# Cross attention of a two-layer decoder, written out as one row of 32 rounds with new bank shares and a later layer norm

## The chip, the cores and the metric

The kernel runs on one core of one Trainium2 chip. The time is the device time of one execution in microseconds (us); the kernel before took 2605.74 us, the median of three runs (2604.7 to 2606.8). An engine takes its instructions strictly in the order in which they stand in its own queue and waits on semaphores for the others. TensorE (PE; PEld is its loading of weights) multiplies into eight banks of PSUM, each 128 x 512 fp32; ScalarE (ACT) and VectorE (DVE) read the banks; GpSimd (POOL) works in SBUF only; SyncE (SP) issues the DMAs.

## The reference

Four sequences of 512 tokens of width 512 pass six blocks, each `x = layernorm(x + f(x))`. The fifth is the one touched:

```
# x [4, 512, 512], ctx [4, 512, 256]; 16 heads of width 128
q = (x @ Wq).reshape(B, Sq, H, D);  k = (ctx @ Wk).reshape(...);  v = (ctx @ Wv).reshape(...)
q = rmsnorm(q, gq);  k = rmsnorm(k, gk)
attn = softmax(einsum('bqhd,bkhd->bhqk', q, k) / sqrt(D))
out = einsum('bhqk,bkhd->bqhd', attn, v).reshape(B, Sq, H * D) @ Wo
x = layernorm(x + out)
```

## The kernel before, in words

The stages run one after another, with a barrier of all engines between. `cross_attention` takes two heads at a time: 8 groups of heads for each of 4 sequences, 32 rounds. Its precision comes from splitting: each fp32 operand is a high part (fp32r, a ScalarE copy) and a low part (the difference), and `split3` (L196) makes three products hi*hi, hi*lo, lo*hi.

A round has these parts, named as the changed code names them:

- **Q**: queries of 2 x 128 columns, two banks of 2 x 256, 24 products each. ScalarE squares and copies each bank (L1833, L1836); VectorE sums the squares (L1909) and scales the result (L1912); GpSimd raises it to -1/2 (L1799, "rstd"); VectorE multiplies q by it (L1919).
- **KV**: keys and values, four tiles; ScalarE empties each in three instructions, squares, k, v (L1844, L1847, L1848). The keys' rstd enters as the scale of the exponential.
- **TQ, TK**: q and k of each head turned by TensorE (L2014, four 128 x 128 transposes to a bank), high part by ScalarE (L1853), low part by VectorE (L1939, L1942).
- **E**: scores, four tiles of 128 keys for each head; ScalarE's exponential goes to SBUF (L1862). No maximum is subtracted, a bound from the gains stands in for it.
- **U, SU**: GpSimd adds the head's four tiles (L1808, L1810), TensorE adds over partitions by a product with ones (L2038).
- **V**: the values times the probabilities (L2031). **R**: VectorE takes the reciprocal of the sum and multiplies the bank of V by it (L1925, L1928).
- **OH**: high and low part of that (L1874, L1932). **O**: four tiles of the output projection, added to x by VectorE (L1958).
- **W**: weights of the next but one round: a DMA into a raw tile, high part by ScalarE, low part by GpSimd (L1792).

The order is written by hand, as the body of a loop that works on round y and on the projections of round y+1: E of both heads, V0, Q0, SU0, V1, SU1, Q1, KV, O0, TK, TQ, O1 to O3. Hardware loops (`turns`, L1734) go over sequences and groups. Q, KV, TK, TQ and xT share banks 0 to 2 in turn, E and O banks 3 to 5, the sums use 3 and 4, V has 6 and 7. At each new sequence `start` turns x (loaded into `x_cur` by a DMA) and splits it, and splits the context; `finish` makes the layer norm on VectorE (L1978, `dve_normalize`, L334).

Of the kernel before, what the change touches and what calls it, by code (L numbers as in the profile page):

```python
# [1632 lines left out]
def cross_attention(c):  # L1633
# [8 lines left out]
    nc, d = c.nc, c.d  # L1642
    HP = 2
    G = 16 // HP
    NW = HP * DX
    with ExitStack() as ctx:
        def sb(nm, shape, dt=F32):
            return ctx.enter_context(nc.sbuf_tensor(f"s5_{nm}", shape, dt))

# [21 lines left out]
        sq = sb("squares", [P, T, NW])  # L1671
# [11 lines left out]
        consts = c.sem("s5_gains_loaded")  # L1683
        bound_ready = c.sem("s5_bound_ready")
        rawx_in = Count(c.sem("s5_w_proj_loaded"), 48)
        rawo_in = Count(c.sem("s5_w_out_loaded"), 16)
        wx_hi = Count(c.sem("s5_w_proj_hi_ready"), 1)
        wx_lo = Count(c.sem("s5_w_proj_lo_ready"), 1)
        wo_hi = Count(c.sem("s5_w_out_hi_ready"), 1)
        wo_lo = Count(c.sem("s5_w_out_lo_ready"), 1)  # L1690
        ctx_in = Count(c.sem("s5_ctx_loaded"), 16)
        ctx_hi = Count(c.sem("s5_ctx_hi_ready"), 1)
        ctx_lo = c.s5_ctx_lo
        squared = {"q": Count(c.sem("s5_q_squared"), 1), "k": Count(c.sem("s5_k_squared"), 1)}
        ms_ready = {"q": Count(c.sem("s5_q_mean_sq_ready"), 1), "k": Count(c.sem("s5_k_mean_sq_ready"), 1)}
        rs_ready = {"q": Count(c.sem("s5_q_rstd_ready"), 1), "k": Count(c.sem("s5_k_rstd_ready"), 1)}
        q_normed = Count(c.sem("s5_q_normed"), 1)
        f_hi = {"qT": Count(c.sem("s5_qT_hi_ready"), HP), "kT": Count(c.sem("s5_kT_hi_ready"), HP)}
        p_sum = Count(c.sem("s5_probs_summed"), HP)
        inv_ready = Count(c.sem("s5_inv_sums_ready"), HP)  # L1700
        o_hi = Count(c.sem("s5_out_hi_ready"), HP)


        pa, pb = c.ps.part(), c.ps.part()
        pa_keys = [("q", 0), ("q", 1)] + [("kv", t) for t in range(T)] + [("kT", 0), ("kT", 1), ("qT", 0), ("qT", 1)]
        pa.open([(k, i % 3, 1) for i, k in enumerate(pa_keys)], outer=c.x_uses([0, 1, 2]))
# [12 lines left out]
        def load_proj(sp, g):
            sp.dma_start(raw_x[:, OQ:OKV].rearrange("p (k n) -> p k n", k=KD),  # L1720
                         d["l1x_wq"].rearrange("(k p) n -> p k n", p=P)[:, :, bass.ds(g * NW, NW)]).then_inc(rawx_in.sem, 16)
            kv = raw_x[:, OKV:].rearrange("p (k a n) -> p k a n", k=KC, a=2)
            for a, nm in ((0, "l1x_wk"), (1, "l1x_wv")):
                sp.dma_start(kv[:, :, a, :],
                             d[nm].rearrange("(k p) n -> p k n", p=P)[:, :, bass.ds(g * NW, NW)]).then_inc(rawx_in.sem, 16)

        def load_out(sp, g):
            sp.dma_start(raw_o[:, :].rearrange("p (h n) -> p h n", h=HP),
                         d["l1x_wo"].rearrange("(h p) n -> p h n", p=P)[:, bass.ds(g * HP, HP), :]).then_inc(rawo_in.sem, 16)

        def turns(eng, start, body, finish):

            start(0)
            body(0, (0, 0), None)  # L1734
            with eng.Fori(0, B - 1) as b:
                with eng.Fori(0, G - 1) as g:
                    body(b, (b, b * G + (g + 1)), b * G + g)
                start(b + 1)
                body(b, (b + 1, b * G + G), b * G + (G - 1))
                finish(b)  # L1740
            b = B - 1
            with eng.Fori(0, G - 1) as g:
                body(b, (b, g + (b * G + 1)), g + b * G)
            body(b, None, b * G + (G - 1))
            finish(b)

        @block.sync
        def _(sp):
            sp.dma_start(gains[:, 0, :], d["l1x_gq"].broadcast_to([P, DX])).then_inc(consts, 16)
# [3 lines left out]
            load_proj(sp, 0)  # L1753
            load_out(sp, 0)

            def next_proj(turn, g):

                sp.wait_ge(*wx_lo.after(turn, 1))
                load_proj(sp, g)

            def next_out(turn, g):
                sp.wait_ge(*wo_lo.after(turn, 1))
                load_out(sp, g)

            def load_sequence(b):
                c.sync_load_x(sp, b)

                sp.wait_ge(*ctx_lo.after(b, 0))
                sp.dma_start(cT[:, :, :], d["ctxT"][bass.ds(b, 1)].rearrange("a (k p) s -> p (a k) s", p=P)) \
                  .then_inc(ctx_in.sem, 16)  # L1770

            load_sequence(0)
            next_proj(0, 1)
            with sp.Fori(0, B - 1) as b:
                load_sequence(b + 1)
                with sp.Fori(0, G - 1) as g:
                    next_out(b * G + g, g + 1)
                    next_proj(b * G + g + 1, (g + 2) % G)
                next_out(b * G + (G - 1), 0)
                next_proj(b * G + G, 1)  # L1780
            with sp.Fori(0, G - 1) as g:
                next_out(g + (B - 1) * G, g + 1)
                next_proj(g + ((B - 1) * G + 1), (g + 2) % G)
            next_out(B * G - 1, 0)

        @block.gpsimd
        def _(pool):
            def lo(out, raw, hi, hi_ready, done, turn, piece=None):

                pool.wait_ge(*hi_ready.after(turn, 1))  # L1790
                pool.wait_ge(c.pool_consts, 1)
                pool.tensor_tensor(out, raw, hi.bitcast(F32), ALU.subtract).then_inc(done.sem, 1)  # L1792

            lo(wx_l[:, 0, :], raw_x[:, :], wx_h[:, 0, :], wx_hi, wx_lo, 0)
            lo(wo_l[:, 0, :], raw_o[:, :], wo_h[:, 0, :], wo_hi, wo_lo, 0)

            def rstd(j, nm, turn):
                pool.wait_ge(*ms_ready[nm].after(turn, 1))
                pool.tensor_tensor(rs[:, j, :, :], ms[:, j, :, :],  # L1799
                                   c.mhalf[:, 0:T * HP].rearrange("p (t h) -> p t h", h=HP), ALU.pow) \  # L1800
                    .then_inc(rs_ready[nm].sem, 1)

            def body(b, x, y):
                if y is not None:
                    for h in range(HP):

                        pool.wait_ge(*pb.released(y, ("e", h, T - 1)))
                        pool.tensor_tensor(psum2[:, :, :], probsT[:, h, 0:2, :], probsT[:, h, 2:4, :], ALU.add)  # L1808
                        pool.drain()
                        pool.tensor_tensor(psum1[:, h, :], psum2[:, 0, :], psum2[:, 1, :], ALU.add).then_inc(p_sum.sem, 1)  # L1810
                        pool.drain()
                if x is not None:
                    tx = x[1]
                    rstd(0, "q", tx)
                    rstd(1, "k", tx)
                    lo(side(wx_l, tx + 1), raw_x[:, :], side(wx_h, tx + 1), wx_hi, wx_lo, tx + 1)
                if y is not None:
                    lo(side(wo_l, y + 1), raw_o[:, :], side(wo_h, y + 1), wo_hi, wo_lo, y + 1)

            turns(pool, nothing, body, lambda b: c.pool_rstd(pool, b))  # L1820

        @block.scalar
        def _(act):
            act.wait_ge(*rawx_in.after(0, 48))
            act.activation(wx_h[:, 0, :], raw_x[:, :], ACT.Copy).then_inc(wx_hi.sem, 1)  # L1825
            act.wait_ge(*rawo_in.after(0, 16))
            act.activation(wo_h[:, 0, :], raw_o[:, :], ACT.Copy).then_inc(wo_hi.sem, 1)
# [839 lines left out]
```

## Time and profile before

| | |
|---|---|
| median of three runs | 2605.74 us |
| the profiled execution | 2605.14 us, span 2603.3 us, 1.8 us lie around it |
| mean granted TensorE clock | 0.942 |
| busy share of the span | PE 84%, DVE 54%, ACT 47%, POOL 35% |
| cross attention | from about 1165.6 to 2300.0 us of the span |

Times in the rows are us from the span's start. In the timeline, neighbouring instructions of one kind stand in one row (x8): its time is that from the first one's start to the last one's end. The bracket at the end is idle time of the engine before the row, and what ended it. Ends of matmuls are modelled: the distance between starts tells what one takes. "128x1024<-128x1024 fp32" is partitions x elements. The granted clock is 1.00 at 2.4 GHz and 0.50 at 1.2 GHz.

### The profile page before, as it was taken

The page shows a single profiled execution, that of the slowest core. Times are in us where ns is not written, and L with a number is a line of the kernel's source. Part 1 is how long each engine was busy: PE and PEld are TensorE (multiplying, and loading weights), DVE is VectorE, ACT ScalarE, POOL GpSimd, SP SyncE. Part 2 cuts the span into 40 slices and gives each one's busy share as a digit, 9 for nine tenths or more (in the row PEclk, how much of TensorE's full clock was granted, in tenths as well). Part 3 has the DMA queues.
Part 4 walks back from the last instruction along what each step waited for, and adds up shares of the span by engine and source line. Part 5 has one row for each costly group of instructions (what it writes and reads, how often), then busy time and mean ns, then how long its engine had stood idle before and what let it go on. Part 6 is the DMA issues. An engine that isn't in the chain of part 4 may idle for free. (4 is left out here: it accounts for less than half of the span.)

```text
span 2603.3 us, 36130 instructions
## 1 busy us (share of the span) xinstructions
PE 2198.1 (84%) x12629; PEld 1560.4 (60%) x12664; DVE 1411.4 (54%) x2138; ACT 1210.6 (47%) x2272; POOL 909.4 (35%) x569
## 2 busy tenths in 40 slices
PE   6989989857876788877999999999999999957672
PEld 4555656446765655546777777776777677734241
DVE  4666666545544544543555755566555655543445
ACT  3645455433325644534555555554555455422323
POOL 3524243410003201203555555544555555510101
PEclk9999999988897999998999999999999999978795
DMA  3000000010001000002111211111111111020001
GB/s 108 2 1 1 1 1 1 1 61 1 1 11 37 1 1 1 1 11 106 48 48 48 73 45 40 39 69 48 48 48 48 49 48 48 32 96 1 1 1 65
DMA packets 62367, 84.15 MB, mean 32 GB/s; under 512 B 6132, under 2 KB 41332, under 8 KB 61752
## 3 DMA queue, kind: packets, MB, share of 16 engines
q1 hardware_dynamic: 62264, 82.76, 9.4%
q8 instruction: 67, 1.10, 0.2%
q14 instruction: 36, 0.29, 0.0%
HBM read 74.36 MB, written 4.19 MB: 30 GB/s over the span
## 5 line engine op out<-in xcount | busy, mean ns | idle before, releaser
L1925 DVE RECIPROCAL s_inv_sums<-banks 128x512 f32<-128x512 f32 x64 | 214.7, 3355 | 342.9 <-PE banks L2038 339.5
L1799 POOL TENSOR_TENSOR s_qk_rstd<-s_mean_sq,minus_half 128x8 f32<-128x8 f32 x64 | 118.6, 1853 | 503.5 <-DVE s_mean_sq L1912 503.5
L2031 PE MATMUL banks<-s_probsT,s_v 128*128 128x512 f32 x512 | 230.2, 592 | 0.0
L1862 ACT ACTIVATE s_probsT<-banks,s_minus_bound,s_qk_rstd 128x512 f32<-128x512 f32 x256 | 177.3, 781 | 93.5 <-PE banks L200 89.5
L594 DVE TENSOR_REDUCE s_neg_max<-banks 128x1 f32<-128x512 f32 x256 | 165.3, 684 | 87.8 <-PE banks L660 86.3
L543 ACT ACTIVATE s_probsT<-banks 128x512 f32<-128x512 f32 x256 | 148.6, 600 | 81.7 <-PE banks L674 79.2
L198 PE MATMUL banks<-s_w_proj_hi,xT_hi 128*128 (+1 forms) x512 | 170.8, 334 | 2.9 <-DVE s_ctxT_lo L1973 2.9
L1833 ACT ACTIVATE s_squares<-banks 128x512 f32<-128x512 f32 x64 | 38.2, 597 | 288.9 <-PE banks L200 288.9
L2031 PEld LDWEIGHTS banks<-s_probsT,s_v 128*128 128x128 f32 x512 | 97.1, 190 | 110.0 <-issue 107.4
L1792 POOL TENSOR_TENSOR s_w_proj_lo<-s_w_proj_raw,s_w_proj_hi 128x2048 f32 (+1 forms) x33 | 152.0, 4605 | 13.9 <-ACT s_w_proj_hi L1825 13.9
L1808 POOL TENSOR_TENSOR s_probs_pair_sums<-s_probsT 128x1024 f32<-128x1024 f32 x64 | 150.9, 2359 | 7.2 <-issue 7.2
L199 PE MATMUL banks<-s_w_proj_lo,xT_hi 128*128 (+1 forms) x512 | 145.8, 285 | 0.0
L200 PE MATMUL banks<-s_w_proj_hi,xT_lo 128*128 (+1 forms) x512 | 145.7, 285 | 0.0
L482 POOL TENSOR_TENSOR x_cur<-s_probsT 128x512 f32<-128x512 f32 x64 | 81.9, 1280 | 156.7 <-PE banks L692 110.1
L660 PE MATMUL banks<-s_kT,s_qT 128*128 128x512 f32 x256 | 117.8, 464 | 6.9 <-ACT s_qT L532 3.3
L198 PE MATMUL banks<-s_wqkv_hi,xT_hi 128*128 128x512 f32 (+1 forms) x256 | 91.9, 359 | 34.5 <-POOL s_wqkv_lo L464 8.8
L674 PE MATMUL banks<-s_qT,s_kT 128*128 128x512 f32 x256 | 106.5, 416 | 16.1 <-ACT s_qT L536 14.0
L198 PEld LDWEIGHTS banks<-s_w_proj_hi,xT_hi 128*128 128x128 f32 x512 | 99.0, 193 | 18.1 <-issue 18.1
L198 PE MATMUL banks<-s_w_out_hi,s_outT_hi 128*128 (+1 forms) x256 | 104.4, 408 | 5.8 <-DVE s_outT_lo L1932 5.8
L199 PEld LDWEIGHTS banks<-s_w_proj_lo,xT_hi 128*128 128x128 f32 x512 | 99.1, 193 | 14.8 <-issue 14.8
L198 PE MATMUL banks<-s_w_proj_hi,s_ctxT_hi 128*128 (+1 forms) x256 | 101.8, 398 | 6.9 <-ACT s_v L1848 6.9
L1958 DVE TENSOR_TENSOR x_all<-banks,x_all 128x512 f32 (+1 forms) x128 | 85.5, 688 | 38.7 <-PE banks L200 35.5
(409 smaller groups left out, 5907.9 us busy)
## 6 DMA issues: line engine op xcount, KB each, us to landing
s_w_proj_raw<-l1x_wq SPq DMA_DIRECT2D x33, 512.0 KB, 4.7
s_w_out_raw<-l1x_wo SPq DMA_DIRECT2D x33, 512.0 KB, 3.6
s_w_proj_raw<-l1x_wk SPq DMA_DIRECT2D x33, 256.0 KB, 4.8
s_w_proj_raw<-l1x_wv SPq DMA_DIRECT2D x33, 256.0 KB, 5.2
x_all<-x SPq DMA_DIRECT2D x4, 1024.0 KB, 12.2
s_ctxT<-ctxT SPq DMA_DIRECT2D x8, 512.0 KB, 6.0
x_cur<-x_all SPq DMA_DIRECT2D x4, 1024.0 KB, 7.8
out<-x_all SPq DMA_DIRECT2D x4, 1024.0 KB, 4.3
```

The lines of the kernel that those rows point to most:

```text
L198: pe.matmul(out, lhs[0], rhs[0], start=start, stop=False)
L199: pe.matmul(out, lhs[0], rhs[1], start=False, stop=False)
L200: return pe.matmul(out, lhs[1], rhs[0], start=False, stop=stop)
L543: act.activation(probsT[:, h % NPB, k, :], ps.ap(s), ACT.Exp).then_inc(ps.freed(s), 1)
L594: dve.tensor_reduce(nmax[:, h % 2, t, 0:1], ps.ap(s), AX.X, ALU.max, negate=True) \
L660: pe.matmul(ps.ap(s), qT[:, h % NQB, t * P:(t + 1) * P], kT[:, h % NKV, :], start=True, stop=True).then_inc(ps.filled(s), 1)
L1792: pool.tensor_tensor(out, raw, hi.bitcast(F32), ALU.subtract).then_inc(done.sem, 1)
L1799: pool.tensor_tensor(rs[:, j, :, :], ms[:, j, :, :], c.mhalf[:, 0:T * HP].rearrange("p (t h) -> p t h", h=HP), ALU.pow) \
L1808: pool.tensor_tensor(psum2[:, :, :], probsT[:, h, 0:2, :], probsT[:, h, 2:4, :], ALU.add)
L1862: act.activation(probsT[:, h, k, :], pb.ap(("e", h, k)), ACT.Exp, bias=bound[:, 0:1], scale=rs[:, 1, k, h:h + 1]).then_inc(pb.freed(("e", ...
L1925: dve.reciprocal(inv[:, h, :], pb.ap(("sum", h))).then_inc(pb.freed(("sum", h)), 1)
L2031: mm = pe.matmul(pb.ap(("o", h)), v[:, k, h * DX:(h + 1) * DX], probsT[:, h, k, :], start=(k == 0), stop=(k == T - 1))
```

## The change

`cross_attention` alone is changed. The loops are gone: a list `seq` holds the steps of all 32 rounds, j = -1 to 32, and every engine walks through it and takes its own part. The parts stand in another order: Q0 comes between the scores of the two heads, TQ comes before TK and between the KV tiles, and OH and O are those of the round before (j - 1). The banks are dealt anew: Q, KV, TK, TQ and half of xT have banks 0 and 1; E, O and the other half of xT have 2 to 4; V has 5 and 6; the sums have bank 7 alone. Squares and probability sums move into `x_cur`, since x is now turned straight from `x_all`; GpSimd's sum is three additions of 512 columns in place of one of 1024 and one of 512. The projection weights' load, high and low part are split in two, WQ and WK. The first DMAs are Wq, the context and Wk/Wv, then the gains, then Wo; Wq's first low part is VectorE's. The layer norm's statistics come with the last additions, and its scaling a round later on ScalarE (LX).

```
+        seq = [("X", 0, k) for k in range(KD)] + [("WQ", 0), ("Cx", 0), ("WK", 0)]
+        for j in range(-1, N + 1):
...
+            if now:
+                seq += [("E", j, 0, k) for k in range(T)] + [("U", j, 0)]
+            if nxt:
+                seq.append(("Q", j + 1, 0))
+            if now:
+                for k in range(T):
+                    seq.append(("E", j, 1, k))
+                    if prv and k < HP:
+                        seq.append(("OH", j - 1, k))
+                seq += [("U", j, 1), ("V", j, 0)]
...
+                seq += [("Q", j + 1, 1), ("MQ", j + 1)]
+            if now:
+                seq += [("SU", j, 0), ("R", j, 0)]
+            if j + 2 < N:
+                seq.append(("WK", j + 2))
+            if now:
+                seq.append(("WO", j))
+            if border:
+                seq += [("X", (j + 2) // G, k) for k in range(KD)]
+            if j % G == 1 and j > G:
+                seq.append(("LX", j // G - 1))
+            if prv:
+                seq.append(("O", j - 1, 0))
+            if nxt:
+                seq.append(("NQ", j + 1))
+            if now:
+                seq.append(("V", j, 1))
+            if nxt:
+                seq.append(("KV", j + 1, 0))
+            if now:
+                seq += [("SU", j, 1), ("R", j, 1)]
+            if nxt:
+                seq += [("KV", j + 1, 1), ("TQ", j + 1, 0), ("KV", j + 1, 2)]
+            if prv:
+                seq.append(("O", j - 1, 1))
+            if nxt:
+                seq += [("TQ", j + 1, 1), ("KV", j + 1, 3), ("MK", j + 1)]
...
+            if s[0] in ("Q", "KV", "TK", "TQ") or s[0] == "X" and s[2] % 2:
+                uses.append((s, na % 2, 1))
+                na += 1
+            elif s[0] in ("E", "O", "X"):
+                uses.append((s, 2 + nb % 3, 1))
+                nb += 1
+            elif s[0] == "V":
+                uses.append((s, 5 + s[2], 1))
+            elif s[0] == "SU":
+                uses.append((s, 7, 1))
...
+                elif ph == "U":
+                    h = s[0]
+                    pool.wait_ge(*ps.released(0, ("E", j, h, T - 1)))
+                    if j > 0:
+                        pool.wait_ge(*ps.full(0, ("SU", j - 1, h)))
+                    pool.tensor_tensor(psum[:, h, :], probs[:, h, 0, :], probs[:, h, 1, :], ALU.add)
+                    pool.drain()
+                    pool.tensor_tensor(psum[:, h, :], psum[:, h, :], probs[:, h, 2, :], ALU.add)
+                    pool.drain()
+                    pool.tensor_tensor(psum[:, h, :], psum[:, h, :], probs[:, h, 3, :], ALU.add).then_inc(p_sum.sem, 1)
...
+                elif ph == "LX":
+                    act.wait_ge(*nmr_ready.after(j, 1))
+                    for t in range(T):
+                        xt = c.x[:, j * T + t, :]
+                        act.activation(xt, xt, ACT.Identity, bias=nmr[:, t:t + 1], scale=c.rstd[:, t:t + 1])
```

MQ and MK are the sum of squares and its small scaling on VectorE with the rstd on GpSimd, NQ is the multiplication of q by its rstd.

**TensorE, the projections ahead of round 0.** L198 is the first product of a tile or of a part of it, L2014 and L2026 are transposes. First before, from the last KV tile on (its further products are left out):

```order
L198 MATMUL banks<-s_w_proj_hi,s_ctxT_hi 128x512 [waits bank2_freed]
...
L2014 MATMUL banks<-ident_sb,s_k 128x128 [waits bank0_freed,bank2_freed]
L2014 MATMUL banks<-ident_sb,s_k 128x128 x3
L2014 MATMUL banks<-ident_sb,s_k 128x128 [waits bank1_freed]
L2014 MATMUL banks<-ident_sb,s_k 128x128 x3
L2014 MATMUL banks<-ident_sb,s_q 128x128 [waits bank2_freed,s5_q_normed]
L2014 MATMUL banks<-ident_sb,s_q 128x128 x3
L2014 MATMUL banks<-ident_sb,s_q 128x128 [waits bank0_freed]
L2014 MATMUL banks<-ident_sb,s_q 128x128 x3
```

and now, from the second KV tile on:

```order
L198 MATMUL banks<-s_w_proj_hi,s_ctxT_hi 128x512 [waits bank1_freed]
...
L2026 MATMUL banks<-ident_sb,s_q 128x128 [waits bank0_freed,s5_q_normed]
L2026 MATMUL banks<-ident_sb,s_q 128x128 x3
L198 MATMUL banks<-s_w_proj_hi,s_ctxT_hi 128x512 [waits bank1_freed]
...
L2026 MATMUL banks<-ident_sb,s_q 128x128 [waits bank0_freed]
L2026 MATMUL banks<-ident_sb,s_q 128x128 x3
L198 MATMUL banks<-s_w_proj_hi,s_ctxT_hi 128x512 [waits bank1_freed]
```

The transposes of q stand between the KV tiles, and KV1, KV2 and KV3 all take bank 1, with one transpose set between KV1 and KV2.

**VectorE, one round from the sum of q's squares on.** Before, in the loop's body (ISA and REGISTER_ALU rows compute semaphore values):

```order
L1909 TENSOR_REDUCE s_mean_sq<-s_squares 128x8 [waits s5_q_squared]
L1912 TENSOR_SCALAR s_mean_sq<-s_mean_sq 128x8
L1931 ISA
L1932 TENSOR_TENSOR s_outT_lo<-s_inv_sums,s_outT_hi 128x512 [waits s5_out_hi_ready]
L1931 REGISTER_ALU
L1932 TENSOR_TENSOR s_outT_lo<-s_inv_sums,s_outT_hi 128x512 [waits s5_out_hi_ready]
L1917 ISA [waits s5_q_rstd_ready]
L1919 TENSOR_TENSOR s_q<-s_q,s_qk_rstd 128x1024 [waits bank1_freed]
```

and now:

```order
L1949 TENSOR_REDUCE s_mean_sq<-x_cur 128x8 [waits s5_q_squared]
L1952 TENSOR_SCALAR s_mean_sq<-s_mean_sq 128x8
L1993 RECIPROCAL s_inv_sums<-banks 128x512 [waits s5_out_lo,bank7_filled]
L1996 TENSOR_TENSOR s_inv_sums<-banks,s_inv_sums 128x512 [waits bank5_filled,bank7_freed]
L2006 TENSOR_TENSOR x_all<-banks,x_all 128x512 [waits bank2_filled]
L1976 TENSOR_TENSOR s_q<-s_q,s_qk_rstd 128x1024 [waits bank1_freed,s5_q_rstd]
L1993 RECIPROCAL s_inv_sums<-banks 128x512 [waits s5_out_lo,bank7_filled]
L1996 TENSOR_TENSOR s_inv_sums<-banks,s_inv_sums 128x512 [waits bank6_filled,bank7_freed]
L1983 SCALAR_TENSOR_TENSOR s_qkT_lo<-banks,s_gain_product_column,s_qkT_hi 128x512 [waits s5_qT_hi]
L2006 TENSOR_TENSOR x_all<-banks,x_all 128x512 [waits bank3_filled]
L1983 SCALAR_TENSOR_TENSOR s_qkT_lo<-banks,s_gain_product_column,s_qkT_hi 128x512 [waits s5_qT_hi]
```

Before, both reciprocals stood ahead of the sum of q's squares; now one stands on each side of the multiplication of q.

**GpSimd, one round from the second head's sum on.** Before:

```order
L1808 TENSOR_TENSOR s_probs_pair_sums<-s_probsT 128x1024 [waits bank4_freed]
L1810 TENSOR_TENSOR s_probs_sum<-s_probs_pair_sums 128x512
L1798 ISA
L1799 TENSOR_TENSOR s_qk_rstd<-s_mean_sq,minus_half 128x8 [waits s5_q_mean_sq_ready]
L1799 TENSOR_TENSOR s_qk_rstd<-s_mean_sq,minus_half 128x8 [waits s5_k_mean_sq_ready]
L1790 REGISTER_ALU
L1792 ISA [waits pool_consts_set,s5_w_proj_hi_ready]
L1792 TENSOR_TENSOR s_w_proj_lo<-s_w_proj_raw,s_w_proj_hi 128x2048
```

and now:

```order
L1854 TENSOR_TENSOR x_cur<-s_probsT 128x512 [waits bank7_filled,bank4_freed]
L1856 TENSOR_TENSOR x_cur<-x_cur,s_probsT 128x512
L1858 TENSOR_TENSOR x_cur<-x_cur,s_probsT 128x512
L1835 TENSOR_TENSOR s_w_proj_lo<-s_w_proj_raw,s_w_proj_hi 128x1024 [waits s5_w_q_hi]
L1829 TENSOR_TENSOR s_qk_rstd<-s_mean_sq,minus_half 128x8 [waits s5_q_mean_sq]
L1839 TENSOR_TENSOR s_w_proj_lo<-s_w_proj_raw,s_w_proj_hi 128x1024 [waits s5_w_kv_hi]
L1843 TENSOR_TENSOR s_w_out_lo<-s_w_out_raw,s_w_out_hi 128x1024 [waits s5_w_out_hi]
L1829 TENSOR_TENSOR s_qk_rstd<-s_mean_sq,minus_half 128x8 [waits s5_k_mean_sq]
```

The weights' low parts stood behind both rstds; now they stand around q's rstd and ahead of k's.

## Rows read from the trace of the kernel before

**Rows 1.** Busy by stretch: us, busy (instructions) of PE, PEld, DVE, ACT, POOL, clock, DMA.
```profile
1241.00:1441.00 200.00, 196.76 (x938) 148.28 (x937) 111.08 (x115) 104.95 (x192) 106.98 (x49) 1.00 0.14 47
```

**Rows 2.** Timeline of ScalarE, the exponentials: start, us, names, idle before.
```profile
1241.73 5.54 ACT L1862 ACTIVATE s_probsT<-banks,s_minus_bound,s_qk_rstd 128x512 f32<-128x512 f32 x8 [3.16 <-PE banks L200]
1275.10 5.54 ACT L1862 ACTIVATE s_probsT<-banks,s_minus_bound,s_qk_rstd 128x512 f32<-128x512 f32 x8 [3.17 <-PE banks L200]
...
2263.04 5.51 ACT L1862 ACTIVATE s_probsT<-banks,s_minus_bound,s_qk_rstd 128x512 f32<-128x512 f32 x8 [3.22 <-PE banks L200]
```

**Rows 3.** Timeline of TensorE, parts of rounds.
```profile
1192.68 0.28 PE L198 MATMUL banks<-s_w_proj_hi,xT_hi 128*128 128x256 f32 x1
1193.04 0.39 PE L198 MATMUL banks<-s_w_proj_hi,s_ctxT_hi 128*128 128x512 f32 x1
1193.73 0.39 PE L198 MATMUL banks<-s_w_proj_hi,s_ctxT_hi 128*128 128x512 f32 x1
...
2240.50 1.02 PE L2038 MATMUL banks<-s_probs_sum,ones_sb 128*128 128x512 f32 x2
2241.36 3.60 PE L2031 MATMUL banks<-s_probsT,s_v 128*128 128x512 f32 x8
2244.79 1.02 PE L2038 MATMUL banks<-s_probs_sum,ones_sb 128*128 128x512 f32 x2
...
2254.09 0.40 PE L198 MATMUL banks<-s_w_out_hi,s_outT_hi 128*128 x1
...
2255.48 1.04 PE L2014 MATMUL banks<-ident_sb,s_k 128*128 128x128 f32 x8
2256.36 0.60 PE L2014 MATMUL banks<-ident_sb,s_q 128*128 128x128 f32 x4
2257.49 0.66 PE L2014 MATMUL banks<-ident_sb,s_q 128*128 128x128 f32 x4 [0.54 <-DVE s_qkT_lo L1942]
```

**Rows 4.** Waits of TensorE in the cross attention: total us, times, longest.
```profile
PE banks L2014 <- DVE s_qkT_lo L1942: 17.3, 32, 0.5
```

**Rows 5.** Timelines of ScalarE and of weight loads, behind the KV tiles of a late round.
```profile
2254.29 0.38 ACT L1844 ACTIVATE s_squares<-banks 128x256 f32<-128x256 f32 x1 [0.30 <-PE banks L200]
...
2255.35 0.93 PEld L2014 LDWEIGHTS banks<-ident_sb,s_k 128*128 128x128 f32 x8
```

**Rows 6.** Timeline of VectorE in the same round.
```profile
2245.85 3.36 DVE L1925 RECIPROCAL s_inv_sums<-banks 128x512 f32<-128x512 f32 x1
2249.24 0.69 DVE L1928 TENSOR_TENSOR s_inv_sums<-banks,s_inv_sums 128x512 f32<-128x512 f32 x1
2249.85 1.21 DVE L1909 TENSOR_REDUCE s_mean_sq<-s_squares 128x8 f32<-128x1024 f32 x1
...
2253.59 1.23 DVE L1919 TENSOR_TENSOR s_q<-s_q,s_qk_rstd 128x1024 f32<-128x1024 f32 x1 [1.04 <-POOL s_qk_rstd L1799]
```

**Rows 7.** Timeline of GpSimd, late rounds.
```profile
2233.94 2.36 POOL L1792 TENSOR_TENSOR s_w_out_lo<-s_w_out_raw,s_w_out_hi 128x1024 f32 x1
...
2261.11 1.65 POOL L1799 TENSOR_TENSOR s_qk_rstd<-s_mean_sq,minus_half 128x8 f32<-128x8 f32 x1 [7.67 <-DVE s_mean_sq L1912]
```

**Rows 8.** Timelines of VectorE and GpSimd at a change of sequence.
```profile
1445.28 2.00 DVE L1973 TENSOR_TENSOR s_ctxT_lo<-s_ctxT,s_ctxT_hi 128x1024 fp32r<-128x1024 f32 x1 [0.26 <-ACT s_ctxT_hi L1892]
1446.13 3.40 POOL L1792 TENSOR_TENSOR s_w_out_lo<-s_w_out_raw,s_w_out_hi 128x1024 f32 x1
...
1481.55 1.17 DVE L330 TENSOR_SCALAR ln_var_eps<-ln_mean_var 128x4 f32<-128x4 f32 x1
...
1486.01 8.05 DVE L334 TENSOR_SCALAR x_all<-x_all,ln_mean_var,ln_rstd  x4 [3.29 <-POOL ln_rstd L339]
```

**Rows 9.** Timeline of TensorE, start of the cross attention and of the next stage.
```profile
1178.00 3.70 PE L283 MATMUL banks<-ident_sb,x_cur 128*128 128x128 f32 x16 [19.10 <-DMA x_cur<-x_all]
1203.21 0.49 PE L198 MATMUL banks<-s_qkT_hi 128*128 128x512 f32 x1 [0.69 <-DVE s_qkT_lo L1939]
...
2300.01 1.30 PE L2487 MATMUL banks<-ident_sb,x_all 128*128 128x128 f32 x5 [7.35 <-PEq L1646]
```

More of the change, by code:

```diff
@@ L1727, in load_out @@
[L1727 to L1745, printed above, removed]
+        nmr = sb("ln_minus_mean_rstd", [P, T])
@@ L1784, in _ @@
[L1784 removed]
+            load_out(0)
+            for ph, j, *s in seq:
+                if ph == "WQ" and j + 1 < N:
+                    sp.wait_ge(*wq_lo.after(j, 1))
+                    load_q(j + 1)
+                elif ph == "WK" and j + 1 < N:
+                    sp.wait_ge(*wk_lo.after(j, 1))
+                    load_kv(j + 1)
+                elif ph == "WO" and j + 1 < N:
+                    sp.wait_ge(*wo_lo.after(j, 1))
+                    load_out(j + 1)
+                elif ph == "Cx" and j + 1 < B:
+                    sp.wait_ge(*ctx_lo.after(j, 1))
+                    load_ctx(j + 1)
@@ L1786, in _ @@
+            sp.wait_ge(consts, 64)
         @block.gpsimd
         def _(pool):
[L1788 to L1818, printed above, removed]
@@ new lines, in _ @@
+            for ph, j, *s in seq:
+                key = (ph, j, *s)
+                if ph == "X":
+                    turned(key, lambda t: c.x[:, j * T + t, s[0] * P:(s[0] + 1) * P])
+                elif ph == "Q":
+                    i = s[0]
+                    if i == 0:
+                        pe.wait_ge(*wq_lo.after(j, 1))
+                        if j % G == 0:
+                            for k in range(KD):
+                                pe.wait_ge(*ps.released(0, ("X", j // G, k)))
+                    ps.wait_empty(pe, 0, key)
@@ L2041, in project_out @@
-                def project_out(t):
-                    pb.wait_empty(pe, y, ("y", t))
-                    for h in range(HP):
-                        mm = split3(pe, pb.ap(("y", t)), (o_h[:, h, t * P:(t + 1) * P], o_l[:, h, t * P:(t + 1) * P]),
-                                    tuple(side(a, y)[:, h * D:(h + 1) * D] for a in (wo_h, wo_l)), h == 0, h == HP - 1)
-                    mm.then_inc(pb.filled(("y", t)), 1)
-                if y is not None:
-                    scores(0)
-                    scores(1)
-                    values(0)
@@ L2052, in body @@
-                if x is not None:
-                    queries(0)
-                if y is not None:
-                    sums(0)
-                    values(1)
-                    sums(1)
-                if x is not None:
-                    queries(1)
-                    for t in range(T):
-                        keys_values(t)
-                if y is not None:
-                    pe.wait_ge(*wo_lo.after(y, 1))
-                    for h in range(HP):
-                        pe.wait_ge(*pb.released(y, ("o", h)))
-                    project_out(0)
@@ L2068, in body @@
-                if x is not None:
-                    transposed("kT", kk, pa.released(x, ("kv", T - 1)))
-                    transposed("qT", q, q_normed.after(x[1], 1))
-                if y is not None:
-                    for t in range(1, T):
-                        project_out(t)
-            def start(b):
-                c.pe_turn_x(pe, b, (b, b * G), pa)
-            turns(pe, start, body, nothing)
-        pa.close(B * G, B)
-        pb.close(B * G)
-        c.close_common()
+                                        (side(wx_h, j)[:, w], side(wx_l, j)[:, w]), k == 0, k == KD - 1)
```

506 lines of the change are left out of this document (279 added, 227 removed).

## The prediction

> **What bounds the kernel now.** I read four views in turn. First the busy time by stretch: from 1241 to 1441 us, six rounds of the cross attention, TensorE is busy 196.8 of 200.0 us at a granted clock of 1.00, while VectorE, ScalarE and GpSimd are at a little over half [rows 1]. So this stage is bound by TensorE, and a new order can win only TensorE's idle time. Second the timeline of ScalarE: the eight exponentials of a round begin 33.4 us apart (1241.73 to 1275.10), and the 30 rounds from 1241.73 to 2263.04 take 1021.3 us [rows 2]. Thirty rounds of 33.36 are 1000.8, so 20.5 us belong to the three changes of sequence. Third the timeline of TensorE inside a round. A three-pass product of 512 columns takes 0.68 to 0.69, one of 256 columns 0.36, eight transposes 0.88 (2255.48 to 2256.36; four so 0.44), a head's values 3.43, a head's sum 0.86 [rows 3]. The query tiles are measured whole. For a round that is: 8 score tiles (E) 5.45, 2 query tiles (Q) 5.74, 4 key/value tiles (KV, 0.695 a product) 5.56, 4 output tiles (O) 5.46, 4 sets of transposes (T) 1.76, 2 V 6.86, 2 sums (SU) 1.72, together 32.55. The round takes 33.36, so 0.81 is idle. Fourth the waits: it is one wait, of the fourth transpose set for the bank of the first key set, 32 times [rows 4]; the third and fourth sets start 1.13 apart where 0.44 would do [rows 3].
>
> **The steady round of the changed kernel.** The products are the same, 32.55. I lay them out in the new order from t = 0 at a round's first score: E(0) to 2.73, Q0 to 5.60, E(1) to 8.32, V0 11.75, Q1 14.62, SU0 15.48, O0 16.84, V1 20.27, KV0 21.66, SU1 22.52, KV1 23.91. Against it I put each consumer, with 0.20 us from the point at which a last product counts as over to ScalarE's start (2254.09 to 2254.29 [rows 3, 5]). Durations given without rows stand in the same timelines.
>
> *Fourth score of the second head, +0.13.* ScalarE now empties Q0 first (5.80; its two instructions take 0.97), so that head's first exponential runs from 6.77 to 7.55. The fourth tile needs that bank, and its weight load may start 0.1 after. A load after a wait costs another 0.11. Its product starts at 7.78, not 7.65. Everything behind shifts by 0.13.
>
> *Third KV tile, +0.93.* Now Q, KV and the transposes share two banks, before three. KV2 takes KV1's bank with only one transpose set (0.44) between. Before, the load that waits for a KV tile to be emptied starts at 2255.35, 1.26 after that tile's 2254.09 [rows 3, 5]; with the 0.11 it is 1.37. 1.37 - 0.44 = 0.93. Before, two tiles (2.8) lay between, and it cost nothing.
>
> *VectorE's chain and GpSimd.* Behind Q1 (end 14.75, squares ready at 15.54) VectorE runs: reduction 1.21 and small scaling, reciprocal 3.36 and product 0.69, O0's addition 0.68, then the scaling of q, then the second reciprocal and product, then the first low part of qT [rows 6]. GpSimd starts the second head's sum when its last exponential ends. That is at 10.6: from 6.77, three more exponentials at a spacing of 0.68 (eight take 5.54 [rows 2]) and two copies at 0.52 lie before its end. The sum is now three additions, each 1.41 as two such of stage 1, so to 14.8. Then come three low parts of weights of 2.36 each, with the rstd (1.65) after the first [rows 7].
> Here is the place that decides. The trace shows that VectorE and GpSimd shut each other out in some pairs. The context's low part, alone 1.22, took 2.00 when it began at 1445.28 beside a GpSimd subtraction that ended at 1446.19, and the next GpSimd subtraction took 3.40, not the 2.36 of one at 2233.94; a tiny VectorE scaling at 1481.55 took 1.17, not 0.17, and ended with GpSimd's subtraction at 1482.7 [rows 7, 8]; while xT_lo, which reads a bank, kept its 0.69 in the same stretch. In the kernel before, the scaling of q (1.23) met no GpSimd tensor operation: GpSimd lay idle in the 7.67 us up to 2261.11, and it ran at 2253.59 [rows 6, 7].
> Now: the first low part runs 14.95 to 17.3 and holds VectorE's small scaling (due 16.9) until 17.35. Both engines start from there. GpSimd: rstd to 19.1, KV weights' low part to 21.4, output weights' low part 21.4 to 23.75. VectorE: 3.39 + 0.61 + 0.68, so the scaling of q is due at 22.05, 0.65 inside the last of them. It then ends about 1.1 after GpSimd does, as at 1447.28 against 1446.19: 24.85, not 23.3. The second reciprocal and product (4.0) end at 28.9, the low part of qT (0.75) at 29.6. TQ1, which needs its bank, is due at 28.15 (KV2 from 25.40, O1 behind) and starts at 29.71: +1.56. Behind it nothing else is late: E of the next round needs kT's low part 0.1 before it is due.
> Round: 32.55 + 0.13 + 0.93 + 1.56 = 35.17, against 33.36: **+1.8 us, times 30 rounds = +54**.
>
> The bounds: with no exclusion the chain ends at 27.6 and the last term is 0 (33.6 a round); if the small scaling alone is held, 0.3 (33.9). Above, a wait for a whole further subtraction (2.36) would give 37.5; the order gives GpSimd none to put there. I take 1.56, since the pair is of the same kind as the one at 1445.28, both inputs in SBUF.
> The Trainium skill ("SBUF — State Buffer", SBUF: two separate sides) says the same of this pair: a VectorE operation with two SBUF inputs, or in a two-port mode, and a GpSimd operation that reads SBUF hold the shared ports exclusively. It speaks against this change, because by it the scaling of q must wait; a reader who allows only what rows show has one operation of that form (four runs of it) as evidence. By the page the sum is the one above, without it 33.6 to 33.9.
>
> **Changes of sequence, -14.5.** Before they cost 20.5 over the rounds. Gone are the ctx wait, and the layer norm on VectorE: four scalings took 8.05 us beside GpSimd's sums at 1486.01 [rows 8] and so the next reciprocal began only at 1493.98; now ScalarE does them (0.80 each at the end of the stage before). New: 16 transposes 1.76, KV0 waiting for an xT bank that VectorE frees at 22.8 (+0.76), bn_stats among the additions (0.75 each, +0.85 at the round's end); in the round with xT the scaling of q falls behind GpSimd's work and saves about 1.4. Together about 2.0 each, 6.0 in all.
>
> **Start, -7.** Before, TensorE waits 19.1 us for x_cur's transfer until 1178.00, then starts Q at 1184.64 and the scores at 1203.21 [rows 9]; the first exponential starts only at 1207.25, after its rstd. Now x is turned straight from x_all at about 1166. But VectorE waits first for the gains, now issued behind 1.5 MB: 1169.1 + 3.9 (as 1166.92 to 1170.78) = 1173, four low parts to 1176.7, Wq's low part 1.22, so Q at 1178.0, 6.6 earlier. Two banks and the missing work between then cost: TQ1 0.5, KV3 0.4, TK 1.3 and E 1.1, so scores at 1199.6, -3.6. Round 0 took 37.6 (1203.21 to 1240.8, which is the exponentials' 1241.73 less 0.9 for the first tile and the latency). It now lacks O (-5.5) but waits for TQ1, TK0 and E: about 34.2, so -3.4.
>
> **End, -1.5.** Before, 37.9 from 2262.1 (2263.04 less 0.9) to the next stage's 2300.01 [rows 2, 9], with TensorE idle for the sums and for 5.77 us before O, whose first product took 0.77. Now the 31st round's O fills the first gap, but the last O still waits for both reciprocals, o_hi also for O of round 30: to about 28.0, then 2.3 for addition and statistics, 1.2, and 2.9 for ScalarE's four scalings instead of 1.9: with some 1.3 for a slow clock and 0.3 to the next stage, 36.4.
>
> **Nothing:** the loops' branches (products go on at 0.68 spacing over the edge), the DMAs (each weight load has half a round), the third addition of the sums (GpSimd at 55%).
>
> **Sum**, on the profiled execution's own 2605.1: +54 - 14.5 - 7 - 1.5 = +31, **2636 us**; the median of the runs is 2605.7, so the two bases are the same.
>
> **Rivals.** A: *the scaling of q is not held* (it gets the port first, or the order slips past GpSimd's last subtraction). Steady 33.9 at most, +16; changes of sequence -13.5, start and end -9.5: 2598, at 33.6 a round 2590. For it: a margin of 0.65 us built from a dozen durations; against it: VectorE and GpSimd both start from the same event, so errors before it cancel. This is the case on the other side, not slower; it decides where q's scaling is due before 21.4. B: *the two-bank wait too is absent*, with A: 32.7, 2563; against it only the measured 1.37. C: *TensorE's clock*: idle 2.6 a round instead of 0.8 could drop it. After the idle stretches ahead of 1207 the products took 0.43 each in place of 0.23; nine of them a round are +1.8, so 2692. Against: its waits are at most 1.6 us long, and the idle stretches around 1207 were longer (3.1 between two loads). D: *the start gains nothing* because the gains land later: 2640, inside the forecast.
>
> **Numbers.** Forecast (with D) 60%, own range 2620 to 2650; A 27%; B 3%; C 4%; the rest, 6%, between A and the forecast, when only part of the rounds are held. A change under 0.2% (5.2 us) can't be told from none. Faster (under 2600.5): three fifths of A and B, 19%; same (to 2611): 12%; slower: 69%. Range 2594 to 2652.
>
> **What would show it.** Rounds of exponentials 35.2 apart (33.6 to 33.9: A). The multiplication of s_q by s_qk_rstd at about 2.8 us instead of 1.23, beside s_w_out_lo; s_mean_sq's scaling 0.6 instead of 0.17 for q, 0.17 for k. TensorE waiting twice a round: KV for ScalarE's s_v (0.9), transposes of s_q for VectorE's s_qkT_lo (1.5). Scores from 1200. If q's scaling is 1.23, the largest term is wrong.

## The result, and the profile after

| | before | changed |
|---|---|---|
| median | 2605.31 us (4 runs) | 2637.36 us (4 runs, 2635.6 to 2640.56) |
| ratio | | 1.0124, interval 1.0109 to 1.0138 |
| profiled execution's span | 2603.3 | 2638.7 |
| scores of round 0 start | 1203.21 | 1204.88 |
| round 0 | 37.6 | 33.75 |
| steady round | 33.36 | 35.13 |
| rounds 1 to 30 | 1021.3 | 1060.2 |
| last round to the next stage | 37.9 | 36.4 |

The change costs 32 us; 2636 was forecast. The profiled execution, 2640.56, is the slowest of the four, so the working below, made on its trace, has 35.4 to explain (2638.7 less 2603.3) and not 32. The steady rounds of the changed kernel lie between 35.10 and 35.20; 35.13 stands for them.

The changed kernel's busy time in the same stretch as [rows 1] (columns as there):

```profile
1241.00:1441.00 200.00, 189.73 (x899) 139.19 (x898) 114.95 (x108) 102.14 (x189) 106.76 (x65) 1.00 0.15 48
```

TensorE's clock is 1.00 as before and it is idle for 10.3 of 200 us, before for 3.2. The first four exponentials of two neighbouring rounds, ScalarE's timeline, against [rows 2]:

```profile
1274.82 2.78 ACT L1922 ACTIVATE s_probsT<-banks,s_minus_bound,s_qk_rstd 128x512 f32<-128x512 f32 x4 [0.19 <-PE banks L200]
...
1309.92 2.78 ACT L1922 ACTIVATE s_probsT<-banks,s_minus_bound,s_qk_rstd 128x512 f32<-128x512 f32 x4 [0.19 <-PE banks L200]
```

They stand 35.1 apart. TensorE's waits in the cross attention, against [rows 4]:

```profile
PE banks L2026 <- DVE s_qkT_lo L1983: 33.3, 27, 1.4
PE banks L2026 <- DVE s_q L1976: 26.7, 27, 4.5
```

The one short wait of before has become two, 27 times each: the second transpose set of q waits for its bank, and the first for q itself. The changed kernel's timelines of VectorE, of GpSimd and of TensorE late in that round, against [rows 6, 7]:

```profile
1291.05 0.20 DVE L1952 TENSOR_SCALAR s_mean_sq<-s_mean_sq 128x8 f32<-128x8 f32 x1 [0.43 <-issue]
1291.16 3.35 DVE L1993 RECIPROCAL s_inv_sums<-banks 128x512 f32<-128x512 f32 x1
...
1295.15 0.68 DVE L2006 TENSOR_TENSOR x_all<-banks,x_all 128x512 f32<-128x512 f32 x1
1295.75 2.97 DVE L1976 TENSOR_TENSOR s_q<-s_q,s_qk_rstd 128x1024 f32<-128x1024 f32 x1
```

```profile
1288.83 2.39 POOL L1835 TENSOR_TENSOR s_w_proj_lo<-s_w_proj_raw,s_w_proj_hi 128x1024 fp32r<-128x1024 f32 x1 [0.16 <-issue]
...
1292.93 2.37 POOL L1839 TENSOR_TENSOR s_w_proj_lo<-s_w_proj_raw,s_w_proj_hi 128x1024 fp32r<-128x1024 f32 x1
1295.26 2.38 POOL L1843 TENSOR_TENSOR s_w_out_lo<-s_w_out_raw,s_w_out_hi 128x1024 fp32r<-128x1024 f32 x1
```

```profile
1298.78 0.66 PE L2026 MATMUL banks<-ident_sb,s_q 128*128 128x128 f32 x4 [0.74 <-DVE s_q L1976]
...
1303.43 0.66 PE L2026 MATMUL banks<-ident_sb,s_q 128*128 128x128 f32 x4 [1.21 <-DVE s_qkT_lo L1983]
```

The scaling of q (s_q by s_qk_rstd) is issued 0.5 us into GpSimd's last subtraction and takes 2.97 in place of 1.23. That is what "held" means below: the instruction shows as a long one and not as a wait. It ends at 1298.72, 1.08 after the subtraction's end at 1297.64. GpSimd loses nothing (2.38), and VectorE's instructions that read a bank (the reciprocal at 3.35, the addition at 0.68) run through GpSimd's subtractions at their own speed.

The last round that projects has no projection weights left to split, and so holds its own control. GpSimd's one subtraction, that of Wo, ends at 2286.43, 0.48 ahead of the scaling; the scaling is short, the first set of q doesn't wait, and the third KV tile waits for its bank. GpSimd, VectorE, then TensorE:

```profile
2284.07 2.36 POOL L1843 TENSOR_TENSOR s_w_out_lo<-s_w_out_raw,s_w_out_hi 128x1024 fp32r<-128x1024 f32 x1
```

```profile
2286.91 1.22 DVE L1976 TENSOR_TENSOR s_q<-s_q,s_qk_rstd 128x1024 f32<-128x1024 f32 x1
```

```profile
2289.39 0.60 PE L2026 MATMUL banks<-ident_sb,s_q 128*128 128x128 f32 x4
2290.58 0.50 PE L198 MATMUL banks<-s_w_proj_hi,s_ctxT_hi 128*128 128x512 f32 x1 [0.59 <-ACT s_v L1907]
```

That round takes 33.56, by its exponentials.

TensorE's timeline at the start, against [rows 9] (the next stage begins at 2335.27):

```profile
1180.45 0.58 PE L198 MATMUL banks<-s_w_proj_hi,xT_hi 128*128 128x256 f32 x1 [9.72 <-DVE s_w_proj_lo L1970]
...
1195.72 1.12 PE L2026 MATMUL banks<-ident_sb,s_q 128*128 128x128 f32 x4 [4.46 <-DVE s_q L1976]
...
1204.88 0.50 PE L198 MATMUL banks<-s_qkT_hi 128*128 128x512 f32 x1 [0.98 <-DVE s_qkT_lo L1986]
```

The projections start 4.2 earlier than before (1184.64), but the lead is gone at the scores: 4.5 of it in one wait for q.

### The profile page after: what moved, and what is told of

Read it like the earlier page. It is cut to its first block and busy times, and to the rows that moved or that the text cites. A ratio compares the mean times of both kernels' runs of the same rounds, so it can differ in the third digit from the quotient of the medians.

```text
span 2638.7 us, 33190 instructions
## 1 busy us (share of the span) xinstructions
PE 2207.2 (84%) x12629; PEld 1550.6 (59%) x12664; DVE 1442.9 (55%) x2127; ACT 1228.6 (47%) x2318; POOL 909.0 (34%) x662
## 5 line engine op out<-in xcount | busy, mean ns | idle before, releaser
L1949 DVE TENSOR_REDUCE s_mean_sq<-x_cur 128x8 f32<-128x1024 f32 x64 | 78.1, 1220 | 188.8 <-ACT x_cur L1890 177.5
L198 PE MATMUL banks<-s_w_proj_hi,xT_hi 128*128 128x256 f32 x512 | 158.0, 309 | 9.7 <-DVE s_w_proj_lo L1970 9.7
L2001 DVE TENSOR_TENSOR s_outT_lo<-s_inv_sums,s_outT_hi 128x512 fp32r<-128x512 f32 x64 | 44.7, 700 | 213.3 <-ACT s_outT_hi L1929 213.3
L1854 POOL TENSOR_TENSOR x_cur<-s_probsT 128x512 f32<-128x512 f32 x64 | 82.0, 1282 | 193.1 <-ACT s_probsT L1922 192.9
L1901 ACT ACTIVATE x_cur<-banks 128x256 f32<-128x256 f32 x128 | 49.2, 384 | 208.7 <-PE banks L200 208.6
L199 PE MATMUL banks<-s_w_proj_lo,xT_hi 128*128 128x256 f32 x512 | 145.6, 284 | 0.0
L200 PE MATMUL banks<-s_w_proj_hi,xT_lo 128*128 128x256 f32 x512 | 145.5, 284 | 0.0
L482 POOL TENSOR_TENSOR x_cur<-s_probsT 128x512 f32<-128x512 f32 x64 | 82.0, 1280 | 156.9 <-PE banks L692 110.1
L198 PE MATMUL banks<-s_w_proj_hi,s_ctxT_hi 128*128 128x512 f32 x256 | 130.4, 510 | 4.7 <-ACT s_v L1907 3.5
L198 PE MATMUL banks<-s_wqkv_hi,xT_hi 128*128 128x512 f32 (+1 forms) x256 | 92.3, 360 | 34.6 <-POOL s_wqkv_lo L464 8.8
L1890 ACT ACTIVATE x_cur<-banks 128x512 f32<-128x512 f32 x64 | 38.2, 598 | 178.1 <-PE banks L200 178.1
L198 PE MATMUL banks<-s_w_out_hi,s_outT_hi 128*128 128x512 f32 x256 | 115.5, 451 | 2.6 <-DVE s_outT_lo L2001 2.6
L198 PEld LDWEIGHTS banks<-s_w_proj_hi,xT_hi 128*128 128x128 f32 x512 | 98.8, 193 | 18.7 <-DVE s_w_proj_lo L1970 10.1
```

What stands on the lines that cost most here:

```text
L198: pe.matmul(out, lhs[0], rhs[0], start=start, stop=False)
L199: pe.matmul(out, lhs[0], rhs[1], start=False, stop=False)
L200: return pe.matmul(out, lhs[1], rhs[0], start=False, stop=stop)
L482: pool.tensor_tensor(c.xcur[:, h % 4, :], p[0], p[1], ALU.add)
```

## The experiments

All are edits of the changed kernel; its round is 35.13 and its median 2637.4. "Run 4" is experiment 4. Times of rounds behind round 0 are those between the first exponentials of neighbouring rounds, in the profiled execution. The kernel before had medians of 2605.3 to 2606.5 beside them.

**1. Low part of Wo behind the keys' rstd.**

```
-                elif ph == "WO":            # GpSimd
+                elif ph == "WOlow":         # in seq behind ("MK", j + 1)
                     pool.wait_ge(*wo_hi.after(j, 1))
```

> Changed kernel, but GpSimd makes the low part of the output weights behind the keys' rstd, when VectorE has no operation with two SBUF inputs at work; all else as it was. Theory (VectorE's scaling of q is held until GpSimd's subtraction ends): the scaling takes 1.22 us in place of 2.97; the first transpose set of q no longer waits (1.2 us now); the third KV tile then waits for its bank, 0.95; the second set of q no longer waits (1.4 now). Round 33.6 in place of 35.12, time about 2590. Rival (the scaling is slow for a reason of its own, as its new place beside the DMAs or the new tiles): it stays at 2.97, round 35.1, time 2637.

Measured: 2599.2 us (ratio to before 0.9972, 0.9962 to 0.9983), round 33.61. VectorE's and TensorE's timelines:

```profile
1291.33 1.21 DVE L1978 TENSOR_TENSOR s_q<-s_q,s_qk_rstd 128x1024 f32<-128x1024 f32 x1
```

```profile
1293.44 0.60 PE L2028 MATMUL banks<-ident_sb,s_q 128*128 128x128 f32 x4
1294.62 0.50 PE L198 MATMUL banks<-s_w_proj_hi,s_ctxT_hi 128*128 128x512 f32 x1 [0.59 <-ACT s_v L1909]
```

The place of one GpSimd instruction turns the loss into a small gain. The wait of the third KV tile appears as soon as the first set is on time: its product starts 1.18 after the transposes, where 0.35 is usual without a wait, so 0.83. The second set of q starts at 1297.50 without a wait. The time is 9 above what was expected. The changes of sequence got dearer: the rounds around the first one take 36.05, 34.14 and 34.74, together 4.1 over three steady ones; in the changed kernel it is 2.2. Over the three changes that is 5.5. And the last projecting round, 1.6 shorter than the others in the changed kernel, is no shorter here. Some 2 us stay unexplained.

**2. Three banks for the projections**, three for scores, outputs and sums together.

```
-                uses.append((s, na % 2, 1))
+                uses.append((s, na % 3, 1))
...
-            elif s[0] in ("E", "O", "X"):
-                uses.append((s, 2 + nb % 3, 1))
+            elif s[0] in ("E", "O", "SU", "X"):
+                uses.append((s, 3 + nb % 3, 1))
```

> Changed kernel with the banks dealt as before the change: three for Q, KV, TQ, TK and half of xT, three for E, O, sums and the other half, two for V. Theory: the scaling of q stays at 2.97 and the first set of q waits 1.2 as now; the second set has a bank of its own and doesn't wait (1.4 gone), but KV3 now takes the first set's bank and waits about 1.0 for VectorE's low part. Round 34.7, time about 2625. Rival (the two banks are the whole cost, the held scaling costs nothing): round 32.9, time 2570.

Measured: 2636.7 us, round 34.75, scaling 2.99. The steady round came as reckoned. The time is 12 above what was expected: the 11 us that the rounds save are lost again at the changes of sequence. The first such round takes 39.7. There an output tile, which now takes the bank of the sums, starts 3.3 us late, at 1430.88, when the reciprocal that frees that bank is over; and right behind that idle stretch the granted clock is 0.57 from 1431 to 1435, where the products take 0.43 and not 0.23.

**3. Both.**

> Both edits: low part of the output weights behind the keys' rstd, and three banks for the projections. Theory: scaling 1.22, no wait of the first set, KV2 doesn't wait, KV3 waits 0.3 for the bank of the first set of q. Round 33.0, time about 2572. Rival (the waits are set by VectorE's chain of two reciprocals, whichever bank): round 33.6 as with the first edit alone, 2590.

Measured: 2590.15 us, 18 above what was expected, round 32.98, scaling 1.22. The changes of sequence cost more still: 41.0, 38.0 and 39.6 for their first rounds, and in the first the granted clock is 0.53 from 1421 to 1428. With experiments 1 and 2 this makes a square: late low part 1.52 off the round with two banks, 1.77 with three.

**4. The dose: half a subtraction at the old place, half behind.**

```
+    pool.tensor_tensor(side(wo_l, j)[:, 0:D], raw_o[:, 0:D], side(wo_h, j)[:, 0:D].bitcast(F32), ALU.subtract)
```

> Changed kernel, with the low part of the output weights in two halves of 512 columns: the first at the old place, the second behind the keys' rstd. A dose for the exclusion. Theory (VectorE waits for the end of GpSimd's instruction and then runs at its own speed): the scaling takes 1.8 us (the half ends 0.7 after it is issued, then 1.1); first set of q on time, KV2 waits 0.95, the second set 0.2. Round 33.85, time about 2598. Rival (the two share the port and each runs slower while both run): GpSimd's half takes 1.6 to 1.9 in place of 1.2, the scaling 1.9.

Measured: 2610.2 us, 12 above what was expected, round 34.04. GpSimd's and VectorE's timelines:

```profile
1290.66 1.29 POOL L1845 TENSOR_TENSOR s_w_out_lo<-s_w_out_raw,s_w_out_hi 128x512 fp32r<-128x512 f32 x1
```

```profile
1291.14 1.89 DVE L1980 TENSOR_TENSOR s_q<-s_q,s_qk_rstd 128x1024 f32<-128x1024 f32 x1
```

The half ends at 1291.95 and the scaling at 1293.03, again 1.08 later. GpSimd's 512 columns take 1.29, as does the other half, which stands later (1303.39). So here one engine waits for the other's instruction; they don't share a rate.

**5. The gains no longer ahead of x's low parts on VectorE.**

```
+                    if j == 0:      # behind the context's low part
+                        bounds()    # wait for the gains, product, maximum
```

> Changed kernel, but VectorE waits for the gains and makes the bound only behind the first context's low part, no longer ahead of x's low parts. Theory (the start fell short because VectorE stood until 1175.8 for the gains): the low parts of x start at about 1169, Q at about 1173.7 in place of 1180.5, and everything behind it moves with it, so the scores at 1198.2 and the time 2631. Rival (the stretch ahead of the scores is held by the held scaling of q and the weights, whatever the gains do): Q earlier, scores later than 1202, time 2635 to 2637.

Measured: 2629.3 us, Q at 1173.75, scores at 1198.05, as the theory had it.

**6. The layer norm's scalings back on VectorE.**

> Changed kernel with the layer norm's four scalings back on VectorE, right behind the rstd (the statistics stay with the additions). The prediction gave part of the 14.5 us at the changes of sequence to their leaving VectorE. Theory now: VectorE is idle for 6.6 us ahead of the low parts of the output of the round before, so even scalings of 5 to 8 us beside GpSimd's sums fit; the round in which they stand gets 0 to 0.5 longer, time 2636 to 2639. Rival (as in the kernel before, where they moved the next reciprocal): 2.5 to 4 longer at each of three changes, time 2645 to 2650.

Measured: 2635.7 us; the round with them takes 35.7 as it did with them on ScalarE. VectorE's timeline:

```profile
1523.77 3.87 DVE L2015 TENSOR_SCALAR x_all<-x_all,ln_mean_var,ln_rstd 128x512 f32<-128x512 f32 x4 [0.53 <-POOL ln_rstd L1862]
```

The same four instructions took 8.05 in [rows 8]. Two of the four are held here too, by GpSimd's sum that starts at 1524.57: one by one they take 0.55, 0.54, 1.52 and 1.51. But they stand in a stretch in which VectorE would idle: it still waits 1.22 behind them. In this order their engine is worth nothing; their place is what counts.

**7. ScalarE empties the first query bank later.**

```
+                if mine[i][0] == "Q" and mine[i][2] == 0 and mine[i + 1][0] == "E":
+                    mine[i], mine[i + 1] = mine[i + 1], mine[i]
```

> Changed kernel, but ScalarE empties the first query bank behind the second head's first exponential instead of ahead of it. Theory: the fourth score tile of the second head no longer waits 0.1 for its bank; round 35.04 in place of 35.17, time 2633 to 2634. Rival (VectorE's chain behind Q1 sets the round, so nothing is saved where TensorE waits for it later): round 35.17, time 2637.

Measured: 2660.5 us (1.0211, 1.0193 to 1.0228), round 35.94: both theories wrong. ScalarE's timeline, the last two exponentials of a round whose first one starts at 1273.86; and the same in the changed kernel, where the first one starts at 1274.82:

```profile
1282.81 1.46 ACT L1926 ACTIVATE s_probsT<-banks,s_minus_bound,s_qk_rstd 128x512 f32<-128x512 f32 x2
```

```profile
1282.99 1.46 ACT L1922 ACTIVATE s_probsT<-banks,s_minus_bound,s_qk_rstd 128x512 f32<-128x512 f32 x2
```

The last exponential ends 10.41 after the round's first one starts, in the changed kernel 9.63: the two copies stood in ScalarE's idle time and now stand among the exponentials. GpSimd's whole row starts from that end. It is 0.78 later, the held scaling with it, and the round is 0.81 longer.

**8. GpSimd's sum as in the kernel before**, one addition of 1024 columns and one of 512.

> Changed kernel with GpSimd's sum of a head's four tiles as in the kernel before: one addition of 1024 columns into a tile of its own and one of 512 (2.50 and 1.42 us from start to start), in place of three of 512 (1.43 each). Theory (the round is set by GpSimd's row: last exponential, sum, three low parts, and VectorE's scaling held until its end): the sum is 0.4 shorter, and so is the round, 34.8 in place of 35.17; time 2626. Rival (as the prediction had it, the third addition is hidden since GpSimd is at 55%): round 35.17, time 2637.

Measured: 2630.1 us (2625.1 to 2632.9), round 34.80. A sum that is 0.4 shorter makes the round 0.33 shorter. With run 7 that shows it from both sides: last exponential, sum, three low parts with q's rstd between them, and the held scaling are the row that sets the round.

**9. Everything together.** The late low part, and ahead of round 0 that of round 1's Wk/Wv too; three banks for the projections and three of the four xT banks from them; the gains late; ScalarE's order of run 7; VectorE's second product with V's bank behind q's first low part.

> The changed order with everything that the runs so far point to: low part of the output weights behind the keys' rstd (and, ahead of round 0, that of round 1's key/value weights too), three banks for the projections, three of the four xT banks from them, the gains behind the context's low part, ScalarE's order as in the run on that alone, and VectorE's second product with the bank of V behind q's first low part. Theory: round 32.65 (TensorE's work and a tenth), changes of sequence 3.5 us each, scores from 1196; time about 2564. Rival (VectorE's chain or the clock takes the rest): round 33.0 as with late low part and three banks, time 2578.

Measured: 2564.7 us (0.985, 0.9834 to 0.9867), round 32.95, scores at 1192.7. The time is the expected one, but not by its parts: the round is 0.3 longer than expected and each change of sequence costs about 5 and not 3.5, while the scores start 3.3 earlier. That it came out is luck.

**10. The same without ScalarE's order of run 7.**

> As the version with all the edits, but with ScalarE's order as in the changed kernel (the first query bank emptied ahead of the second head's exponentials). Theory: the last exponential and so GpSimd's sum and first low part end 0.8 earlier in the round, the small scaling of q's mean square is not held, VectorE's chain is ahead by that much, and the wait of KV3 (0.2) goes, while the fourth score's 0.1 comes back: round 32.85 in place of 32.95, time about 2561. Rival (KV3's wait is ScalarE's): round 33.05, 2568.

Measured: 2554.3 us (0.9802, 0.9788 to 0.9815), round 32.75, changes of sequence 34.5, 32.9 and 33.9. TensorE is busy without a gap in the steady stretch (columns as above):

```profile
1270.00:1445.00 175.00, 175.00 (x831) 130.34 (x831) 105.25 (x106) 95.42 (x177) 98.43 (x59) 1.00 0.16 52
```

It beats both kernels. It is 7 better than expected: 3 from a round of 32.75 for 32.85, the rest at the changes of sequence, which I had not laid out for it.

## Why the prediction was right, and where it wasn't

**The steady round: right to 0.04, with one wait misnamed.** Forecast 35.17, measured 35.13; against the gapless 32.75 of run 10 that is 2.4 of waits, where the forecast had 2.5 on top of 32.68. The held scaling (step "VectorE's chain and GpSimd") came as reckoned: 2.97 for 2.8, the end 1.08 after GpSimd's for 1.1, the second set of q late by 1.4 to 1.5 for 1.56. Run 1 takes it away, run 4 shortens it to 1.89, the last projecting round lacks it. The small scaling of q's mean square, forecast at 0.6, took 0.53 to 0.57 in 24 rounds; the 0.20 of the row shown above is one of the exceptions: it was issued 0.17 before the subtraction ended. The Trainium skill ("SBUF — State Buffer", SBUF: two separate sides) has the rule by which a VectorE operation with two SBUF inputs and a GpSimd one that reads SBUF exclude each other; the trace agrees with it, by the 2.97.

The step "third KV tile, +0.93" did not happen as told. That tile doesn't wait; the first set of q does, about 1.0. My own numbers held it: scaling done at 24.85, first set due at 24.04. I followed the late scaling only to the second set and priced the bank alone. While the first set waits, the bank behind it comes free, so the two waits take each other's place and are not added. Run 1 uncovers the bank's 0.83. The sum was right because both come to about the same, 0.93 forecast for the one and about 1.0 measured for the other. That is luck; with a longer hold it would not have been.

**"Nothing: the third addition of the sums (GpSimd at 55%)"** was wrong by 0.33 a round, run 8. An engine that is half idle still sets the round if its row ends in the wait. The durations were in the layout, so the sum didn't suffer; the reason did.

**Changes of sequence, -14.5: measured -14.2 (20.5 to 6.3), partly for another reason.** The 6.3 holds 7.1 at the changes (6.0 forecast), 0.3 in one other round, 0.5 in hundredths of the steady ones, and -1.6 for the last projecting round, which I had counted as a steady one. And the 20.5 of before holds 1.6 that belongs to no change: one round there takes 38.16 where its two fellows take 36.6, with a granted clock of 0.57 from 1504 to 1508. Moving the scalings off VectorE is worth nothing here (run 6). And the low cost is probably in part cover: in run 1, where the steady round has less idle time, the same transposes and statistics cost 4.1 a change and not 2.2. No run isolates that.

**Start, -7: measured +1.7 for the scores' start and -3.9 for round 0.** The former failed (-3.6 forecast); the latter is near its forecast (-3.4), but not for its reasons, see below. Two things are late: VectorE got the gains at 1175.8 and not at 1173, and q's first scaling met GpSimd's low part of round 1's weights. Timelines of GpSimd and VectorE in the changed kernel:

```profile
1192.25 2.34 POOL L1839 TENSOR_TENSOR s_w_proj_lo<-s_w_proj_raw,s_w_proj_hi 128x1024 fp32r<-128x1024 f32 x1
1192.32 3.35 DVE L1976 TENSOR_TENSOR s_q<-s_q,s_qk_rstd 128x1024 f32<-128x1024 f32 x1 [1.75 <-POOL s_qk_rstd L1829]
```

Once more it ends 1.08 after GpSimd does. The first set of q waits 4.5, which the forecast didn't have at all. The hold is 2.1 of it (3.35 for 1.22). The other 2.3 are the chain from Q's banks through the sum of squares and the rstd to that scaling, with only two KV tiles of work for TensorE meanwhile. I had applied the exclusion to the steady round and not here. Run 5 takes the gains away: scores 6.8 earlier, 8 us in the time. Run 9 also moves the low part: the scaling takes 1.23, and that wait falls to 2.5.

Round 0 also holds a drop of the clock that I had not seen coming. Busy time by stretch, from 1204 to 1210, in the changed kernel and in run 1, whose start has the same order but for the low part of Wo:

```profile
1204.00:1210.00 6.00, 5.12 (x18) 4.17 (x19) 1.29 (x2) 3.39 (x6) 1.42 (x1) 0.72 0.00 0
```

```profile
1204.00:1210.00 6.00, 6.00 (x40) 5.40 (x39) 0.07 (x1) 3.31 (x6) 2.45 (x3) 1.00 0.00 0
```

Round 0 takes 33.75 in the first and 32.16 in the second. Run 6 has the same 0.72 and 33.75; runs 4, 5, 7 and 8 have 1.00 and 32.1 to 32.2. Since the scores start 24.4 behind Q's first product in the changed kernel and 25.0 in run 1, about 1 us of the 1.6 is left. One execution of each kernel is profiled, so whether the changed kernel's other ones have the drop is not shown. On this trace the forecast missed the start by 4.8 (-7 for -2.2), and that is its largest error. The median is off by 1 alone, since the profiled execution is 3.2 slower than the median; that is luck too.

**End, -1.5:** 36.4 as forecast. **Sum** on the trace: 30 x 1.77 = 53, -14.2, +1.7, -3.9, -1.5, together 35.2 of 35.4.

Rival A (not held) is excluded by the scaling's 2.97, and run 1 gives what it would have brought: round 33.6, 2599 for the 2590 to 2598 named. B's two-bank wait exists but was covered. D, a start that gains nothing, is nearly what came (-2.2 with round 0), and it stood inside the forecast. C (a lower clock in every round) did not come: 1.00 in the steady rounds, and one drop, in round 0.

What stays open: which of DMA landing and issue order made the gains 2.8 later than reckoned, since no run moved the DMAs; why the clock dropped in round 0 of some traces and not of others; and how the changes of sequence came out so cheap in run 10.

## What to carry to other kernels

Before reordering, lay all engines' rows of one round side by side and mark each VectorE instruction with two SBUF inputs, and each scaling from SBUF to SBUF (runs 6 and 9 show those held too): GpSimd should have no subtraction or addition of its own in that window, or VectorE's instruction waits for the end of it. Carry a late value to its first reader, not only to the next one you had in mind, and don't add waits that lie behind one another. Put weights' splitting and copies where the other engine reads banks or idles; here one moved instruction was worth 38 us.

## What was not expected of the hardware

The hold is exact: in three different places (1298.72 and 1195.67, and 1293.03 in run 4) the scaling ended 1.08 us after GpSimd's instruction, whether it had been issued 0.5 or 0.1 us after that one's start; run alone it takes 1.22. All 28 held scalings of q in the changed kernel ended 1.08 or 1.09 after, also the one at 1227.51, issued 2.2 into a subtraction. Even an operation on 8 columns is held: 0.17 became 1.04 in run 9, where it was issued at 1273.86 beside a subtraction from 1272.49 to 1274.88.
